# First experts, tiles 7 to 15: the sixth low part of a tile moves from GpSimd to VectorE

## The reference

```python
x = x + _L0_conv_ref(_ln_c(x), ...)       # attention over rows and over columns
t = t + _L0_ffn_ref(_ln_t(t), ...)        # first experts
x = x + _L1_conv_ref(_ln_c(x), ...)       # convolution and state space mixer
t = t + _L1_ffn_ref(_ln_t(t), ...)        # second experts
```

```python
h = jax.nn.gelu(jnp.einsum('bsd,edh->ebsh', x, w1) + b1[:, None, None, :], approximate=False)
y = jnp.einsum('ebsh,ehd->ebsd', h, w2) + b2[:, None, None, :]
out = jnp.einsum('bse,ebsd->bsd', masked, y)
```

## Time and profile before

| | us |
|---|---|
| median of 3 runs | 2015.39 |
| lowest, highest | 2012.67, 2019.69 |
| the profiled execution's own time | 2017.45 |
| its span, first to last instruction | 2015.6 |

### The profile page before, as it was taken

The page is one execution under the profiler, slowest core; times in us unless marked ns, Lnnn a source line. Parts: engine busy times, 40 slices in busy tenths (PEclk is TensorE's granted clock), DMA queues, the critical chain, the costliest instruction groups (busy, mean ns, idle before and its releaser), DMA issues. The chain is left out here.

```text
span 2015.6 us, 65496 instructions
## 1 busy us (share of the span) xinstructions
PE 1783.4 (88%) x25822; PEld 1421.5 (71%) x25822; DVE 1601.4 (79%) x5172; ACT 1109.1 (55%) x2203; POOL 1267.7 (63%) x1322
## 2 busy tenths in 40 slices
PE   4877858989999489999999999999999859999996
PEld 3665656667777478888777777777778646777775
DVE  6688788867778658788888898988889878777775
ACT  3444216667777455555554555454554237777774
POOL 3248656888787625445564756566565657777776
PEclk9677679999999789999998999998999869999998
DMA  9320023657555540000000000000000035655554
GB/s 146 104 77 32 28 93 107 198 179 215 179 189 183 147 70 4 4 3 3 7 9 10 12 11 9 11 12 10 9 12 12 14 115 175 201 182 188 183 190 127
DMA packets 95413, 174.31 MB, mean 86 GB/s; under 512 B 53256, under 2 KB 66550, under 8 KB 95108
## 3 DMA queue, kind: packets, MB, share of 16 engines
q10 hardware_dynamic: 21312, 102.00, 15.8%
q1 hardware_dynamic: 56516, 41.86, 8.9%
q0 software_dynamic: 17280, 26.26, 3.8%
HBM read 134.71 MB, written 36.72 MB: 85 GB/s over the span
## 5 line engine op out<-in xcount | busy, mean ns | idle before, releaser
L1176 PE MATMUL ps<-rounded 97*128 97x512 f32 (+4 forms) x952 | 389.0, 409 | 28.7 <-DMA rounded<-weights_by_expert 9.4
L951 ACT ACTIVATE rounded<-ps 128x512 fp32r<-128x512 f32 (+1 forms) x444 | 259.8, 585 | 205.6 <-PE ps L1178 123.0
L1177 PE MATMUL ps<-rounded 97*128 97x512 f32 (+4 forms) x952 | 369.6, 388 | 0.0
L1178 PE MATMUL ps<-rounded 97*128 97x512 f32 (+4 forms) x952 | 369.4, 388 | 0.0
L1268 PE MATMUL ps<-rounded 128*128 128x224 f32 (+1 forms) x2256 | 354.9, 300 | 2.9 <-DVE arena L1389 2.9
L2099 DVE TENSOR_TENSOR rounded<-arena,rounded 128x512 fp32r<-128x512 f32 (+1 forms) x312 | 245.6, 790 | 137.4 <-ACT arena L952 136.8
L1268 PEld LDWEIGHTS ps<-rounded 128*128 128x128 f32 x2256 | 308.8, 201 | 37.6 <-issue 6.5
L952 ACT ACTIVATE arena<-ps 128x512 f32<-128x512 f32 (+1 forms) x444 | 260.1, 586 | 0.0
L770 POOL TENSOR_TENSOR w<-arena,consts 128x384 f32<-128x384 f32 x128 | 107.5, 840 | 221.5 <-DVE arena L1473 221.5
L1176 PEld LDWEIGHTS ps<-rounded 97*128 97x128 f32 (+2 forms) x952 | 167.3, 176 | 90.1 <-issue 14.8
L702 POOL TENSOR_TENSOR rounded<-arena,rounded 128x512 fp32r<-128x512 f32 (+1 forms) x132 | 166.6, 1262 | 85.0 <-ACT arena L952 83.7
(11 more groups left out here) (361 smaller groups left out, 3887.4 us busy)
## 6 DMA issues: line engine op xcount, KB each, us to landing
rounded<-weights_by_expert ACTq DMA_DIRECT2D x148, 673.0 KB, 4.2
arena<-rows SPq DMA_DIRECT2D x68, 208.0 KB, 2.7
residual<-in_x SPq DMA_DIRECT2D x16, 384.0 KB, 7.3
weights_by_expert<-rounded SPq DMA_DIRECT2D x8, 672.0 KB, 3.5
residual<-after_ffn SPq DMA_DIRECT2D x12, 384.0 KB, 6.7
w<-in_w SPq DMA_DIRECT2D x4, 576.0 KB
rows<-arena SPq DMA_DIRECT2D x11, 208.0 KB
after_ffn<-arena POOLq DMA_INDIRECT x142
```

What stands on the lines that cost most here:

```text
L951: act.activation(hidr[:, 0, c, 0:width(t)], bank(UPS[step % len(UPS)])[:, 0:width(t)], ACT.Gelu)
L1176: pe.matmul(dst, left[0], right[0], start=start, stop=False)
L1177: pe.matmul(dst, left[1], right[0], start=False, stop=False)
L1178: return pe.matmul(dst, left[0], right[1], start=False, stop=stop)
```

## The change

`on_pool` returns False for all chunks in tiles 7 to 15 of the first experts. In these nine tiles VectorE makes all six low parts, and GpSimd none; its indirect DMAs stay as they are. Tiles 0 to 6, tiles from 16 on, and the second experts stay as they were. The table `LOWS`, from which TensorE and ScalarE take the count to wait for, follows from `on_pool`.

```diff
 def on_pool(l, t, c):
-    return c == ON_POOL[1] or c == ON_POOL[0] and not (l == 0 and t < EARLY - 2)
+    if l == 0 and 7 <= t < EARLY - 2:
+        return False
+    return c == ON_POOL[1] or c == ON_POOL[0] and not (l == 0 and t < 7)
```

## The result

The changed kernel takes 2006.28 us (median of 8 runs, 1995.76 to 2016.43), the kernel before 2017.53 us (8 runs, 2012.67 to 2019.69). The ratio is 0.9944, with a 95% interval of 0.9924 to 0.9965: faster by 11.3 us, 7.1 to 15.3. The prediction said 2006.4 us and a gain of 9.0. The time is hit more closely than it deserves: the median of before rose from 2015.39 to 2017.53 with more runs, and the gain was 2.3 us larger than forecast; the two made up for each other. The profiled execution took 2005.72 us with a span of 2003.9.

What follows compares the result with a forecast made beforehand. GpSimd's queue was taken to set the pace, TensorE coupled to it by one low part per tile. The queue's 8.25 us plus 0.75 of slack gave 9.0 off 2015.39: 2006.4 us, range 2002.5 to 2012.0.

Steps and rivals of the forecast that it cites:

- TensorE's clock of 9.50 us a tile: First experts' tiles after tile 6: freed of GpSimd, TensorE runs at 9.50 us a tile, 11.8 us ahead by tile 12.
- GpSimd's queue, 11.0 less 2.75 us: Tiles 7 to 15: removed low parts shorten the queue by 11.0 us, stretched DMAs return 2.75, leaving 8.25.
- 0.31 us of stretching for every low part: GpSimd's indirect DMAs: each VectorE low part lengthens them by 0.31 us in all, 2.75 us for nine more.
- VectorE has room: VectorE, tiles 7 to 15: one more 0.69 us low part makes 7.9 to 8.0 us a tile and costs nothing itself.
- What joins the two: Token loads hang on GpSimd's results, so its 8.25 us lead limits TensorE's 11.8, with two tight places.
- Place (a): Tile 16's tokens: load comes 5.1 us earlier (or 4.3), VectorE 7.3 to 8.1 earlier, with 3 us to spare.
- Place (b): Tile 18's tokens: the wait comes forward by 8.25 us and no more; slack adds 0 to 1.5, taken as 0.75.
- Rival 1: Token loads have more slack than assumed, TensorE runs free and all 11.8 us arrive: 2003.6 us; chance 0.15.
- my case: The forecast's main case: a gain of 7 to 10.5 us, 2004.9 to 2008.4 us; chance 0.56.
- Rival 2: GpSimd's DMAs stretch, mean above 1.35 us, and give most back: gain 5.8 us, 2009.6, at worse 2012; chance 0.20.
- Rival 3: Chunk 5's low part stands behind tile 16's token wait; loses from 12 us delay, 2021 us at 18; chance 0.05.
- Rival 4: Nothing happens, because another engine holds the 11.74 us tile: 2015 us; chance 0.04.

Runs made afterwards that it cites:

- pool_short: Kernel before, with GpSimd's low part of chunk 5 in tiles 7 to 15 cut to 8 of 512 columns; stage 360.1 us, TensorE's tile 10.63 us.
- before_again: Kernel before, unchanged, profiled once more for scatter; stage 361.8 us against 367.1 in its first profile, TensorE's tile 11.25 us.
- dve_short: Changed kernel, with VectorE's nine new low parts cut to 8 of 512 columns; stage 352.6 us, GpSimd's tile 9.74 us.
- dve_twice: Changed kernel, with VectorE making chunk 5's low part twice in tiles 7 to 15; stage 359.2 us, GpSimd's tile 9.96 us.
- after_again: Changed kernel, unchanged, profiled once more; stage 354.6 us against 354.7 in its first profile, token waits 10.4 us.
- before_ring7: Kernel before, with seven token buffers in place of six; stage 364.6 us, TensorE's tile 11.26 us.
- dve_twice_again: Changed kernel, with chunk 5's low part made twice on VectorE in tiles 7 to 15, second run; stage 354.5 us, GpSimd's tile 10.19 us.
- only_7_11: Changed kernel, but only tiles 7 to 11 have all low parts on VectorE, tiles 12 to 15 keep chunk 5's on GpSimd; stage 359.5 us.

## Why the prediction was right

- **The bound.** GpSimd's queue, and the one instruction in it that TensorE needs. Shown, by the 9.50 us tiles of the change and by pool_short.
- **TensorE's clock of 9.50 us a tile.** Exact for tiles 10 to 14. The prediction took 11.8 us up to tile 12 from this. From tile 9's input columns to tile 14's the change brought 10.5 us between the first two profiles (58.6 to 48.1) and 7.2 between the second two (54.9 to 47.7): the two tiles from tile 8's columns to tile 10's still took 10.25 and 10.09 us in the first, and before_again had shorter tiles to begin with. This term was too large.
- **GpSimd's queue, 11.0 less 2.75 us.** From tile 6's row block to the last one it took 98.9 us before (95.8 in before_again), 87.9 and 88.6 after. So the queue gained 11.0 in the first pair, 7.2 in the second, 9.1 in the mean, and 8.25 was predicted. The 1.16 us for each removed low part are read from rows and weren't measured by themselves. The step "0.31 us of stretching for every low part" is refuted as a mechanism: dve_short found 0.8 us a tile for removing one, dve_twice a shorter tile for adding one. Between the first two profiles the mean DMA didn't grow (1.208 and 1.196 us), between the second two it did (1.136 and 1.217). That 2.75 us gave a usable sum is in part luck.
- **VectorE has room.** Yes: 31.02 us busy in 38.00, and TensorE undisturbed. But 2 to 3 us came with its new low parts through GpSimd, as dve_short showed; that is near the 2.75 of the sum, and not as a price for each.
- **What joins the two.** The kind of place was named rightly, tokens that come late from the slower queue. Place (a), tile 16's, came in the first profile of the change (5.52 us of waiting; 3.0 was the whole reserve): its load went out 7.3 us earlier than before (461.55 against 468.81), more than the 5.1 reckoned, but VectorE was ready for it 13.1 us earlier (461.84 against 474.95), where 7.3 to 8.1 were reckoned. Place (b), tile 18's, came in after_again (2.62 us). The prediction looked at tiles 16 and 18 only; tiles 13 to 15 waited too, and after_again's longest wait, 4.86 us, was tile 15's. TensorE stood 1.78 + 0.90 us behind these waits in after_again and not at all in the first profile.
- **Sum.** By the stage the change brought 7.1 to 12.5 us, with 9.8 between the means of two profiles each; by the timed medians 11.3, 7.1 to 15.3. The forecast of 9.0 is in both. What happened from tile 14 on was to take 2.8 us back from the 11.8; from tile 14's columns to the last it took 210.7 and 211.1 us with the change, 212.6 and 210.8 without, so next to nothing was given back. A first term that was too large and a loss that hardly came made up for each other. Rival 1 (11.8, TensorE free) is nearer to the timed gain than my 9.0, and 11.3 lies above my case's own 7 to 10.5. As a mechanism it fits the first profile, where no token wait reached TensorE; after_again speaks against it. Rival 2 happened in part: in the second pair the DMAs did stretch, but their mean stayed far from its 1.35. Rival 3's wait happened, at 5.5 us and not at the 12 and more that it needed. Rival 4 is out.

Part of the 12.4 us between the two first profiles, from tile 8's columns to the last, is luck. Around 463 both kernels have TensorE stopped for 2.23 us while the mixer's weights are loaded. In the kernel before, seven of the matmuls that follow, over 3 us, take 0.63 us; in the changed kernel none does. This was not traced to a cause; the change may have a hand in it or not.

## What to carry to other kernels

An engine that is full with work that nobody waits for costs little; put one input of the critical engine into its queue and the whole kernel takes its pace. Taking that input out is worth more than making it shorter, but look next for what still hangs on the slower queue (here the buffers that its results set free), and how many tiles of lag these can carry. Where 0.5% is at stake, a single profile of each kernel can be off by half of that in the very stage that was changed (the kernel before had 367.1 and 361.8 us): take two of each before a price is read from their difference.

## What was not expected of the hardware

- A low part of VectorE (two inputs in SBUF) that met GpSimd's low part took 2.44 us in place of 0.69. Within one execution (before_again, before_ring7) it was now VectorE's instruction that was held, now more of GpSimd's DMAs that were stretched, and a tile took 10.8 or 11.74 us. This closed loop of engines had two ways to run.
- A VectorE low part lengthened an indirect DMA of GpSimd only if it was under way when the DMA began or began within 0.13 us of it (1.25 us in the mean). 0.13 us later it cost nothing (0.98 us, at most 1.01, in 208 cases), and VectorE's own instruction was never longer for it.
- With more VectorE work beside them GpSimd's indirect DMAs were shorter (1.12 and 1.15 us against 1.20 and 1.22), as they were with less of it (1.09).
- A stop of TensorE was followed by matmuls of 0.63 us (the 1.2 GHz level) in the profiles of before (2.23 us), pool_short (2.53), dve_twice (2.55), dve_twice_again (1.95) and only_7_11 (4.03), and by none in the changed kernel, which stopped for 2.23 us as well. The length of the stop alone doesn't tell which comes.
